# Fused image-and-text embedding with two layers on one Trainium2 core: the second half of the ternary down weights is made behind the low part of pair 0's turned rows, and its temporary moves from the squares' tile to the weight stage

## The chip, the cores and the metric

The kernel runs on one core of a Trainium2 chip. The metric is the device time of one execution in microseconds, taken as the median of several executions. The engines are named as the profile names them: PE is TensorE (PEld its weight loads), DVE is VectorE, ACT is ScalarE, POOL is GpSimd and SP is SyncE, which here only issues DMAs.

## What is computed

The reference embeds 32 images and 32 texts, runs a first layer (attention and a ternary feed-forward part) and then a second layer (a recurrent scan and a mixture of experts). The change touches the first layer's feed-forward weights alone:

```python
def _ternary_linear(x, w):
    alpha = jnp.mean(jnp.abs(w))
    w_t = jnp.sign(w) * (jnp.abs(w) > 0.5 * alpha).astype(w.dtype)
    w_q = w + jax.lax.stop_gradient(w_t - w)
    rms = jnp.sqrt(jnp.sum(x * x, axis=-1, keepdims=True)) / jnp.sqrt(jnp.asarray(d, x.dtype))
    return jnp.einsum('bsd,fd->bsf', x / (rms + EPS), w_q)
h = jax.nn.gelu(_ternary_linear(x, w_up), approximate=False)      # w_up: 1024 x 256
return _ternary_linear(h, w_down)                                 # w_down: 256 x 1024
...
h = h + _L0_attn_ref(_layernorm(h, axis=-1), L0_attn_wq, L0_attn_wk, L0_attn_wv)
h = h + _L0_ffn_ref(_layernorm(h, axis=-1), L0_ffn_w_up, L0_ffn_w_down)
```

## The kernel before

Three parts run one after the other: part A is layer 0, part B the recurrent part of layer 1, part C its experts. The change is in part A (`part_a`), which works on 16 pairs of batch elements. A pair is 384 rows of 256 values, held as 3 tiles of 128 rows. Matrices are multiplied as a high and a low part: ACT writes the high part out of PSUM, DVE the difference, and PE multiplies with both.

Each engine runs the same hand-written list of steps, `order` (L169), once per turn `g` of a software pipeline. `run` (L183) walks the list; `offset` says which pair a step works on: offset 0 is pair g, offset 1 (the default) pair g + 1, offset 2 pair g + 2, and steps of pairs that don't exist are left out. The turns -4 to 1 are written out, a hardware loop runs the middle ones, and the last four are written out again. Within an engine the list is the order; between engines only semaphores hold.

The feed-forward weights are made ternary on DVE, in two parts of 1024 columns each (`ternary`, L468). A part is two instructions: L478 writes (-w > threshold) as 0 or 1 into a temporary, `tern_tmp`, and L481 writes (w > threshold) minus that into `ternary_up` or `ternary_down`. `tern_tmp` lies in the first 1024 columns of `gelu_sq`, the tile into which ACT writes the squares of the gelu outputs from turn 0 on. Both parts of the down weights are made in turn -1, one behind the other, between `t_split` (which writes tT_lo of pair 1) and `scale2` (which normalises pair 0's rows for the feed-forward part). PE needs them at `down` of pair 0 in turn 0, where it waits for `w_sum` 4 (L747 to L749).

Around that place the pair 0 rows go this way, through all engines, in turn -1: DVE `scale2` (L664, L667, L671) writes x2_normed; PE `x2T` (L699) turns it into PSUM; ACT `x2_split` (L454) writes x2T_hi, and DVE `x2_split` (L541) x2T_lo. Between them stands DVE's `max` of pair 1 (L601, L605), for which ACT's `exp` of pair 1 (L438) waits, and PE's `tok` of pair 2 too, since it writes over the scores. Turn 0 goes on with `tok` of pair 2 (L688), `pT` of pair 1 (L827, behind ACT's exp) and the first `up` of pair 0 (L688), which needs x2T_lo. DVE's first step in turn 0 is `patch_split` of pair 3 (L537), which waits for tok of pair 2, the reader of patches_hi.

`weight_stage` is a tile of 2048 columns into which the patch weights (columns 0 to 1535) and the value weights (1536 to 2047) land before they are split. Its first 1024 columns are last read by DVE's first L531, at the start of part A. `fill` (L711) has PE do idle transposes at some places of the first turns; none stands ahead of x2T.

Of the kernel before, what the change touches and what calls it, by code (L numbers as in the profile page):

```python
# [71 lines left out]
def part_a(nc, W, io, consts):  # L72
    with ExitStack() as ctx:
        def sb(name, shape, dt=F32):
            return ctx.enter_context(nc.sbuf_tensor(name, shape, dt))
# [5 lines left out]
        stage = sb("weight_stage", [P, 4 * DI])  # L81
# [30 lines left out]
        sq = sb("gelu_sq", [P, DEEP, GT])  # L112
# [3 lines left out]

        flat_act = act[:].rearrange("p a b -> p (a b)")
        wq, wk = (flat_act[:, i * DC * D:(i + 1) * DC * D].rearrange("p (a b) -> p a b", a=DC) for i in range(2))
        tern_tmp = sq[:].rearrange("p a b -> p (a b)")[:, 0:1024]
        vec, soft = sb("channel_vectors", [P, 3, IC]), sb("softplus", [P, 7, IC])  # L120
        ms, rms = sb("rms_mean", [P, TILES]), sb("rms_root", [P, TILES])
        rden, rscale = sb("rms_den", [P, TILES]), sb("rms_scale", [P, TILES])
# [25 lines left out]
        for src, hi, lo in ((io["tokW"], tok_h, tok_l), (io["wvT"], wv_h, wv_l)):  # L148
            cols = flat(hi).shape[1]
            for a in range(0, cols, 1024):  # L150
                b = min(cols, a + 1024)
# [11 lines left out]
        order = """ids_load exp gelu_table tok merge pT up.0 up.1 patch_split patch_load emb pT_split root1 gelu.0 gelu.1 v  # L163
# [4 lines left out]
        order = [(w.split(".")[0], int((w + ".0").split(".")[1])) for w in order]  # L168
# [8 lines left out]
        for m, behind in enumerate((("turn_win", 0), ("up", 4), ("down", 2), ("down", 2), ("down", 2), ("down", 2), ("down", 2), ("down", 2))):  # L177
# [2 lines left out]
                at += 1  # L180
            order_last.insert(at, ("fold", m))

        def run(eng, piece, prepare=None):  # L183


            def step(g, sl, half, order=order):
                if prepare is not None and isinstance(g, int):
                    prepare(g)
                for kind, k in order:
                    off = offset.get(kind, 1)  # L190
                    if not isinstance(g, int) or 0 <= g + off < G:
                        piece(kind, k, g + off, (sl + off) % 2, half + (sl + off) // 2)

            for g in (-4, -3, -2, -1, 0, 1):
                step(g, g % 2, g // 2)
            with eng.Fori(1, G // 2 - 2) as half_:
                step(2 * half_, 0, half_)
                step(2 * half_ + 1, 1, half_)
            for g in range(G - 4, G):
                step(g, g % 2, g // 2, order_last if g == G - 1 else order)  # L200
# [38 lines left out]
        def _(sp):  # L239
# [27 lines left out]
            def piece(kind, k, n, sl, half):  # L267
# [7 lines left out]
                if kind == "h2" and k == TILES - 1:  # L275
                    sp.wait_ge(s["h2_done"], TILES * (n + 1))
                    for j in range(2):
                        sp.dma_start(io["h2"][2 * n + j, 0:N_IMG, :],
                                     h[j * N_IMG:(j + 1) * N_IMG, sl, 0, :]).then_inc(s["stored"], 16)
                        sp.dma_start(io["h2"][2 * n + j, N_IMG:T, :], h[:, sl, 1 + j, :]).then_inc(s["stored"], 16)  # L280

            run(sp, piece, prepare)
            sp.wait_ge(s["rows_out"], 16)
            sp.wait_ge(s["raw_in"], 48)
# [3 lines left out]
        def _(pool):  # L288
# [36 lines left out]
            def piece(kind, k, n, sl, half):  # L325
# [26 lines left out]
                if kind == "root2":  # L352
# [7 lines left out]
                                            ALU.pow).then_inc(s["ln2_roots"], 1)  # L360

            run(pool, piece, prepare)

        @block.scalar
        def _(sc):
# [26 lines left out]
            def piece(kind, k, n, sl, half):  # L392
# [58 lines left out]
                if kind == "x2_split":  # L451
                    sc.wait_ge(s["x2T_done"], n + 1)
                    wait(sc, s["up_done"], FC * n)
                    nc.scalar.activation(x2_h[:], XT[:, :, 0:GT], ACT.Copy).then_inc(s["x2_hi"], 1)  # L454

            run(sc, piece, prepare)

        @block.vector
# [1188 lines left out]
def program(nc, io):  # L1647
    with ExitStack() as ctx:
# [24 lines left out]
        both = ctx.enter_context(ExitStack())  # L1673
        W.ps = both.enter_context(nc.psum_tensor("psAB", [P, 8, 512], F32))
        part_a(nc, W, io, consts)

        E = Names()
# [69 lines left out]
```

## Time and profile before

| | us |
|---|---|
| median of 3 executions | 978.78 |
| lowest and highest of them | 977.89, 979.78 |
| the profiled execution, its own time | 980.27 |
| its span, first to last instruction | 978.5 |
| PE busy in the span | 936.2 (96%) |
| DVE busy | 791.5 (81%) |
| ACT busy | 593.9 (61%) |
| POOL busy | 544.8 (56%) |

A row of the timeline is a group of like instructions: start in us from the span's start, us it took, engine, line, operation, what is written from what, its shape, how many; in brackets the idle time of the engine just before it, with what ended it. PE's rows overlap, as matmuls are pipelined: the distance of their starts is the pace. Names in the profile stand without numbers, so `ln_den` may be ln2_den and `x_normed` may be x2_normed; the lines tell them apart.

### The profile page before, as it was taken

What the parts mean: (1) busy time and instruction counts of PE and PEld (TensorE: products, weight loads), DVE (VectorE), ACT (ScalarE), POOL (GpSimd) and SP (SyncE); (2) the same over time, 40 slices, a digit from 0 to 9 for tenths busy, and PEclk for the clock granted to TensorE, in tenths of its full rate; (3) what the DMA queues carried; (4) which work ended last, traced back from release to release, by engine and by line L of the source; (5) the groups of instructions that cost most, each with busy time, mean ns of one, the idle gap of its engine ahead of it and who ended that gap; (6) DMA issues with size and microseconds to landing.
All of it is one profiled execution on the core that took longest, in us unless ns stands there. A gap on an engine that the chain in (4) does not pass through costs nothing. (4 is left out here: it accounts for less than half of the span.)

```text
span 978.5 us, 19836 instructions
## 1 busy us (share of the span) xinstructions
PE 936.2 (96%) x6016; PEld 838.5 (86%) x6016; DVE 791.5 (81%) x2380; ACT 593.9 (61%) x1182; POOL 544.8 (56%) x674
## 2 busy tenths in 40 slices
PE   6889999999999999988899999999999999998998
PEld 6789999999999999875678888888888888887887
DVE  4878777777877777774589999999999988996787
ACT  2356666666666666664766767666677666752442
POOL 4156666666666776544445545554554466542673
PEclk9999999999999999999999999999999999999999
DMA  6001111111111113003699999999999999984220
GB/s 225 18 28 44 45 44 44 43 43 43 43 43 43 43 39 146 17 17 107 95 145 152 158 151 159 152 151 152 165 156 172 181 164 153 149 136 84 103 65 23
DMA packets 63021, 96.36 MB, mean 98 GB/s; under 512 B 12372, under 2 KB 32988, under 8 KB 62300
## 3 DMA queue, kind: packets, MB, share of 16 engines
q1 hardware_dynamic: 61396, 91.19, 50.4%
q0 software_dynamic: 1536, 4.20, 1.4%
q8 instruction: 37, 0.61, 0.3%
q14 instruction: 44, 0.36, 0.2%
q10 hardware_dynamic: 8, 0.00, 0.0%
HBM read 31.90 MB, written 13.11 MB: 46 GB/s over the span
## 5 line engine op out<-in xcount | busy, mean ns | idle before, releaser
L334 POOL TENSOR_TENSOR gelu_lo<-gelu_out,gelu_hi 128x384 fp32r<-128x384 f32 x124 | 146.0, 1206 | 29.1 <-DVE gelu_hi L549 28.7
L1058 POOL TENSOR_TENSOR B_y<-B_scan_in,B_states 128x512 f32<-128x512 f32 x47 | 60.7, 1291 | 80.2 <-ACT B_states L1147 80.2
L752 PE MATMUL psAB<-ternary_down,gelu_hi 128*128 128x256 f32 x384 | 96.8, 290 | 5.2 <-POOL gelu_lo L334 4.4
L688 PE MATMUL psAB<-x2T_hi,ternary_up 128*128 128x384 f32 x256 | 92.7, 362 | 0.8 <-DVE residual L678 0.6
L752 PE MATMUL psAB<-ternary_down,gelu_lo 128*128 128x256 f32 x384 | 93.3, 281 | 0.0
L688 PE MATMUL psAB<-x2T_lo,ternary_up 128*128 128x384 f32 x256 | 86.2, 337 | 0.0
L1336 PE MATMUL psAB<-Win_hi,B_x_hi 128*128 128x512 f32 x192 | 83.6, 435 | 0.0
L752 PEld LDWEIGHTS psAB<-ternary_down,gelu_hi 128*128 128x128 f32 x384 | 72.2, 188 | 9.6 <-POOL gelu_lo L334 8.0
L1070 POOL TENSOR_TENSOR B_decayed_u<-B_scan_in 128x512 f32<-128x512 f32 x48 | 62.3, 1297 | 29.6 <-DMA B_scan_in<-B_stage 26.6
L1243 DVE SCALAR_TENSOR_TENSOR psAB<-B_decayed_u,psAB 128x128 f32<-128x128 f32 x192 | 67.9, 354 | 13.3 <-PE psAB L1348 11.7
L1348 PEld LDWEIGHTS psAB<-B_partial_dots,B_minus_same_batch 128*128 128x128 f32 x384 | 65.1, 190 | 14.5 <-DVE B_partial_dots L1227 4.4
L1336 PE MATMUL psAB<-Win_hi,B_x_lo 128*128 128x512 f32 x192 | 75.5, 393 | 0.0
L1336 PE MATMUL psAB<-Win_lo,B_x_hi 128*128 128x512 f32 x192 | 75.3, 392 | 0.0
L752 PEld LDWEIGHTS psAB<-ternary_down,gelu_lo 128*128 128x128 f32 x384 | 72.4, 189 | 0.0
L1064 POOL TENSOR_TENSOR B_v_scale<-B_half_vv,half_powers 128x1 f32<-128x1 f32 x48 | 26.5, 551 | 77.9 <-ACT B_v_squared L1168 74.2
L403 ACT ACTIVATE gelu_out<-psAB 128x384 f32<-128x384 f32 x128 | 62.7, 490 | 10.5 <-PE psAB L688 10.2
L1227 DVE CUSTOM_DVE_ANT_0 B_products<-B_scan_in,psAB 128x128 f32<-128x128 f32 x192 | 55.1, 287 | 13.4 <-DVE psAB L1243 7.8
L1232 DVE TENSOR_TENSOR psAB<-psAB,B_scan_in 128x128 f32<-128x128 f32 x192 | 57.5, 299 | 6.5
L568 DVE TENSOR_TENSOR gelu_sq_sum<-gelu_sq_sum,gelu_sq 128x384 f32<-128x384 f32 x105 | 61.1, 582 | 1.7
L1348 PE MATMUL psAB<-B_partial_dots,B_minus_same_batch 128*128 128x1 f32 x384 | 54.6, 211 | 4.0 <-DVE B_partial_dots L1227 3.7
L318 POOL TENSOR_TENSOR patches_lo<-patches,patches_hi 128x768 fp32r<-128x768 f32 x16 | 29.7, 1855 | 50.7 <-DVE patches_hi L537 50.5
L390 ACT ACTIVATE gelu_sq<-gelu_out 128x384 f32<-128x384 f32 x112 | 57.3, 528 | 0.0
(275 smaller groups left out, 3346.2 us busy)
## 6 DMA issues: line engine op xcount, KB each, us to landing
B_scan_in<-B_stage SPq DMA_DIRECT2D x192, 256.0 KB, 6.9
patches<-in_patches SPq DMA_DIRECT2D x16, 384.0 KB, 3.1
B_residual<-layer_out SPq DMA_DIRECT2D x48, 128.0 KB, 4.2
out_dram<-B_residual SPq DMA_DIRECT2D x48, 128.0 KB, 3.6
layer_out<-residual SPq DMA_DIRECT2D x32, 128.0 KB, 1.8
raw_Win<-in_experts SPq DMA_DIRECT2D x3, 768.0 KB, 4.3
raw_Wl<-in_experts SPq DMA_DIRECT2D x3, 768.0 KB, 4.1
layer_out<-residual SPq DMA_DIRECT2D x32, 64.0 KB, 2.0
```

Source lines behind the costliest of these rows:

```text
L334: nc.gpsimd.tensor_tensor(act_l[:, k, :], act[:, k % DEEP, :], act_h[:, k, :].bitcast(F32), ALU.subtract).then_inc(s["ffn_lo"], 1)
L390: nc.scalar.activation(out, act[:, k % DEEP, :], ACT.Square).then_inc(s["sq_done"], 1)
L403: nc.scalar.activation(act[:, k % DEEP, :], ps[:, 6 + k % 2, 0:GT], ACT.Gelu).then_inc(s["gelu_done"], 1)
L568: nc.vector.tensor_tensor(sqsum[:], sqsum[:], sq[:, k % DEEP, :], ALU.add).then_inc(s["sqsum_done"], 1)
L688: last = nc.tensor.matmul(out, a, b, start=(n == 0), stop=(n == len(terms) - 1))
L752: last = nc.tensor.matmul(ps[:, 6 + k // 2, (k % 2) * D:(k % 2 + 1) * D], x[:, c, k * P:(k + 1) * P], dn_w[:, c, :], start=(c == 0 and x i ...
L1058: nc.gpsimd.tensor_tensor(y[:, j % 2], ring[:, j % R_RING, :, GATE, :], hs[:, j % 2], ALU.mult).then_inc(s["y"], 1)
L1070: nc.gpsimd.tensor_tensor(lu[:, j % 2], ring[:, j % R_RING, :, LAM, :], ring[:, j % R_RING, :, U, :], ALU.mult).then_inc(s["lu"], 1)
L1232: nc.vector.tensor_tensor(state(j, k), state(j, k), ring[:, j % R_RING, k, DRIVE, :], ALU.subtract).then_inc(s["scan"], 1)
L1243: nc.vector.scalar_tensor_tensor(out=state(i, k), in0=lu[:, i % 2, k, :], scalar=dot[:, t % 2:t % 2 + 1], in1=state(i, k), op0=ALU.mult, o ...
L1336: last = nc.tensor.matmul(out, a, b, start=(not biased and ks[0] == 0 and n == 0), stop=(ks[-1] == DC - 1 and n == len(terms) - 1), skip_g ...
L1348: nc.tensor.matmul(dot[:, t % 2:t % 2 + 1], minus[:], part[:, t % 2:t % 2 + 1], start=True, stop=True).then_inc(s["dot"], 1)
```

## The change

One extra list, `order_fill`, is `order` with the second part of the down weights, `("tern_down", 1)`, taken out and put at the end. It is used in turn -1 alone, the only turn in which that step does anything. `tern_tmp` becomes the first 1024 columns of `weight_stage`; this holds for all four ternary parts.

```diff
-        tern_tmp = sq[:].rearrange("p a b -> p (a b)")[:, 0:1024]
+        tern_tmp = stage[:, 0:1024]
...
+        order_fill = [w for w in order if w != ("tern_down", 1)] + [("tern_down", 1)]
...
-                step(g, g % 2, g // 2)
+                step(g, g % 2, g // 2, order_fill if g == -1 else order)
```

No instruction is added or taken away, and PE, ACT, POOL and SP have the same lists as before. On DVE, two instructions move. The first place is DVE in turn -1 between tT_lo of pair 1 and pair 0's normalised rows; before:

```order
L541 TENSOR_TENSOR tT_lo<-psAB,tT_hi 128x768
L472 TENSOR_SCALAR half_alpha<-psAB 128x1
L478 TENSOR_SCALAR gelu_sq<-raw_Wv,half_alpha 128x1024
L481 SCALAR_TENSOR_TENSOR ternary_down<-raw_Wv,half_alpha,gelu_sq 128x1024
L478 TENSOR_SCALAR gelu_sq<-raw_Wv,half_alpha 128x1024
L481 SCALAR_TENSOR_TENSOR ternary_down<-raw_Wv,half_alpha,gelu_sq 128x1024
L664 SCALAR_TENSOR_TENSOR ln2_den<-ln2_roots 128x3
```

The same place in the changed kernel (its lines are numbered 3 higher):

```order
L544 TENSOR_TENSOR tT_lo<-psAB,tT_hi 128x768
L475 TENSOR_SCALAR half_alpha<-psAB 128x1
L481 TENSOR_SCALAR weight_stage<-raw_Wv,half_alpha 128x1024
L484 SCALAR_TENSOR_TENSOR ternary_down<-raw_Wv,half_alpha,weight_stage 128x1024
L667 SCALAR_TENSOR_TENSOR ln2_den<-ln2_roots 128x3
```

One of the two pairs of ternary instructions is gone from ahead of ln2_den, the first step of the normalisation.

The second place is DVE at the end of turn -1 and the start of turn 0; before:

```order
L605 TENSOR_SCALAR neg_max<-row_max 128x3
L541 TENSOR_TENSOR x2T_lo<-psAB,x2T_hi 128x768
L537 CAST patches_hi<-patches 128x768
L610 TENSOR_TENSOR embedded<-psAB,patch_bias 128x256
L614 BN_STATS ln_stats<-embedded 128x6 x3
```

And in the changed kernel:

```order
L608 TENSOR_SCALAR neg_max<-row_max 128x3
L544 TENSOR_TENSOR x2T_lo<-psAB,x2T_hi 128x768
L481 TENSOR_SCALAR weight_stage<-raw_Wv,half_alpha 128x1024
L484 SCALAR_TENSOR_TENSOR ternary_down<-raw_Wv,half_alpha,weight_stage 128x1024
L540 CAST patches_hi<-patches 128x768
L613 TENSOR_TENSOR embedded<-psAB,patch_bias 128x256
L617 BN_STATS ln_stats<-embedded 128x6 x3
```

The moved pair now stands between x2T_lo of pair 0 and the split of pair 3's patches.

## Rows read from the trace of the kernel before

**Rows 1.** A window of 25 us: length, busy us of each engine (instructions), PEclk, DMA.

```profile
217.00:242.00 25.00, 24.80 (x186) 24.02 (x186) 19.62 (x57) 16.20 (x35) 17.36 (x17) 1.00 0.15 42
```

**Rows 2.** Timeline of PE, end of turn -1 to the middle of turn 0.

```profile
54.50 1.19 PE L699 MATMUL psAB<-ident,x_normed 128*128 128x128 f32 x6 [3.25 <-DVE x_normed L671]
55.62 0.55 PE L688 MATMUL psAB<-tokW_hi,patches_hi 128*128 128x256 f32 x1
...
59.05 0.71 PE L827 MATMUL psAB<-ident,probs 128*128 128x128 f32 x5
...
65.35 0.28 PE L688 MATMUL psAB<-v_hi,probT_hi 128*128 128x256 f32 x1
```

**Rows 3.** Timeline of DVE over the same stretch.

```profile
50.99 0.75 DVE L478 TENSOR_SCALAR gelu_sq<-raw_Wv,half_alpha 128x1024 f32<-128x1024 f32 x1
...
52.98 0.15 DVE L664 SCALAR_TENSOR_TENSOR ln_den<-ln_roots 128x3 f32<-128x3 f32 x1
...
53.39 1.06 DVE L671 TENSOR_SCALAR x_normed<-residual,ln_moments,ln_scale 128x256 f32<-128x256 f32 x3
...
55.39 0.08 DVE L601 DVE_READ_ACCUMULATOR2_ANT row_max<- 128x1 f32 x1
...
56.57 0.96 DVE L541 TENSOR_TENSOR x2T_lo<-psAB,x2T_hi 128x768 fp32r<-128x768 f32 x1 [0.89 <-ACT x2T_hi L454]
59.31 0.56 DVE L537 CAST patches_hi<-patches 128x768 fp32r<-128x768 f32 x1 [1.79 <-PE psAB L688]
...
62.52 0.60 DVE L549 CAST gelu_hi<-gelu_out 128x384 fp32r<-128x384 f32 x2
64.15 0.96 DVE L541 TENSOR_TENSOR v_lo<-psAB,v_hi 128x768 fp32r<-128x768 f32 x1 [1.03 <-ACT v_hi L379]
```

**Rows 4.** Timeline of ACT: pair 0's high part, pair 1's exp, the table load.

```profile
55.73 0.81 ACT L454 ACTIVATE x2T_hi<-psAB 128x768 fp32r<-128x768 f32 x1 [7.93 <-PE psAB L699]
56.43 0.50 ACT L438 ACTIVATE probs<-probs,neg_max 128x256 f32<-128x256 f32 x1
...
58.02 1.28 ACT L433 ACT_TABLE_LOAD   x1
...
59.79 0.71 ACT L379 ACTIVATE probT_hi<-psAB 128x640 fp32r<-128x640 f32 x1 [0.27 <-PE psAB L827]
```

**Rows 5.** Timeline of POOL: pair 0's roots, then pair 3's low patches.

```profile
47.91 1.76 POOL L359 TENSOR_TENSOR ln_roots<-ln_pair,half_powers 128x6 f32<-128x6 f32 x1
...
59.96 1.86 POOL L318 TENSOR_TENSOR patches_lo<-patches,patches_hi 128x768 fp32r<-128x768 f32 x1 [8.08 <-DVE patches_hi L537]
```

**Rows 6.** Timeline of PE, other places: the same steps at full pace.

```profile
41.88 0.82 PE L699 MATMUL psAB<-ident,x_normed 128*128 128x128 f32 x6
42.53 1.26 PE L716 MATMUL psAB<-ident 128*128 128x128 f32 x10
...
81.79 0.36 PE L688 MATMUL psAB<-tokW_hi,patches_hi 128*128 128x256 f32 x1
...
84.03 0.71 PE L827 MATMUL psAB<-ident,probs 128*128 128x128 f32 x5
```

**Rows 7.** Timeline of PE: three other idle stretches of the first turns.

```profile
10.93 0.35 PE L688 MATMUL psAB<-tokW_hi,patches_hi 128*128 128x256 f32 x1 [1.88 <-DVE tokW_lo L531]
...
21.03 1.33 PE L699 MATMUL psAB<-ident,x_normed 128*128 128x128 f32 x5 [4.24 <-DVE x_normed L628]
...
32.54 0.36 PE L688 MATMUL psAB<-tokW_hi,patches_hi 128*128 128x256 f32 x1 [1.43 <-DVE row_max L601]
```

**Rows 8.** Windows around PE's idle stretches, columns as in rows 1.

```profile
31.00:33.00 2.00, 0.57 (x5) 0.49 (x5) 1.69 (x8) 0.36 (x1) 0.00 (x0) 1.00 0.00 0
...
54.40:58.00 3.60, 3.50 (x17) 3.20 (x18) 2.20 (x9) 2.27 (x7) 0.00 (x0) 0.57 0.00 0
...
490.00:500.00 10.00, 8.38 (x36) 6.59 (x36) 7.18 (x27) 5.38 (x11) 4.03 (x8) 0.83 1.09 151
```

**Rows 9.** Waits of PE's weight loads from 60 to 450 us: total, times, longest.

```profile
PEld psAB L752 <- POOL gelu_lo L334: 8.0, 17, 1.2
```

## The prediction

> **What bounds the kernel now.** I read the table of windows first. In the middle turns PE is busy 24.80 of 25 us, at clock 1.00, while DVE has 19.62 and POOL 17.36 [rows 1]; the windows from 67 to 367 us read alike. So in the steady turns PE is the bound, and whatever makes PE start turn 0 earlier should reach the end of the kernel whole, since every later wait, transfers included, hangs on steps of these turns. What is left to win lies in the first turns, where PE still waits for one pair's chain. The timeline of PE shows the place: the transposes of pair 0's rows start at 54.50, after 3.25 us idle that DVE's x2_normed ended [rows 2]; so the work before, the scores of pair 1, ended at 51.25. DVE is not waiting in that time, it is working: the second ternary part stands at 50.99, ln2_den at 52.98, x2_normed at 53.39 [rows 3]. The idle stretch costs a second time, behind it. PE takes 1.12 us from the first transpose to the first tok matmul (54.50 to 55.62) [rows 2], where the same six transposes take 0.65 (41.88 to 42.53) elsewhere [rows 6]; and the 18 tok matmuls take 3.43 us (55.62 to 59.05) [rows 2] against 2.24 (81.79 to 84.03) [rows 6]. The reason is the granted clock, 0.57 in this window of 3.6 us [rows 8]: the lower level, 1.2 GHz, for nearly all of it.
>
> **Taking the second part out of the front.** It holds DVE from 50.99 to 52.98, that is 1.99 us [rows 3]. With it gone ln2_den can start at 50.99 if its input is there: POOL's roots end at 49.67 (47.91 + 1.76) [rows 5], so nothing else is late, and there is 1.32 us of room. x2_normed starts at 51.40, the row maxima end at 53.48 (55.39 + 0.08 - 1.99) [rows 3], and neg_max, one small instruction, follows. PE's transposes start at 52.51 instead of 54.50, after 1.26 us idle. Shift so far: **1.99 us**.
>
> **The clock.** PE has idled 1.88 and 1.43 us elsewhere in these turns [rows 7], and the window around the latter shows clock 1.00 [rows 8]; the tok matmuls behind it run at the full pace. After 4.24 us the transposes were slow, five in 1.33 us [rows 7], and after 3.25 us they were slow too [rows 2]. A gap of 1.26 us is nearest to the first two, so I take the full clock. The two ends are 0 (the clock falls all the same) and the whole difference. At the full clock: transposes 52.51 to 53.16. tok of pair 2 must wait for the row maxima, which end at 53.48; behind the same wait the matmul came 0.14 us later in the rows I have (55.47 to 55.62) [rows 2, 3], so it starts at 53.62 and its 18 matmuls end at 53.62 + 2.24 = 55.86. pT also needs ACT's exp. x2T_hi started 1.23 us after the first transpose at the slow pace [rows 2, 4]; less the 0.47 that the transposes save, it is at 52.51 + 0.76 to 0.86 = 53.3 to 53.4, the exp follows 0.70 later at 54.1 (it stood behind x2T_hi without idle time, not behind neg_max), and ends 1.59 later (56.43 to 58.02) [rows 4], at 55.7. So pT starts at 55.86 instead of 59.05: **shift 3.19 us**, with exp 0.1 to 0.2 us ahead of being the bound. The clock's part is 1.2 us of it.
>
> The Trainium skill ("TensorE: Matmul & The Clock Gate", Part 1) says that the monitor that gates the clock is free-running and that its transition point differs from one execution of a kernel to the next. No row here can show that, since one execution was profiled. By it the 3.25 us gap may leave the clock up in some executions of the kernel before, and for those the change would bring only the first term; the second rival below has that time.
>
> **What the part costs in its new place.** x2T_lo waits for x2T_hi as before and runs from about 54.2 to 55.1. Then the part takes its 1.99 us, to 57.1, on a stretch where DVE used to stand idle 1.79 us for tok of pair 2 (57.5 to 59.31) [rows 3]. At the full clock tok is done at 55.9, so patches_hi of pair 3 is now late by DVE's own work: 57.1 instead of 56.1, a shift of 2.2 us where PE has 3.2. What queues behind it on DVE: embedded and its moments, probT_lo, the first gelu_hi, then v_lo, for which PE's pv waits. DVE had 1.03 us idle ahead of v_lo (waiting for v_hi) [rows 3]; the lag is 1.0 us. So gelu_hi ends at 63.12 - 2.2 = 60.9 and v_hi, shifted 3.2, ends at 64.15 - 3.2 = 60.95: v_lo comes on time to within 0.1 us, and pv (65.35) [rows 2] had v_lo at 65.11, another 0.2 us of room. I take 0 for it; the end on the other side is 0.3. POOL's patches_lo follows patches_hi (59.96) [rows 5] and is read a turn later. ACT's probT_hi stood 0.27 us idle and then at 59.79 [rows 4]; now the table load ends at 55.7 + 1.49 = 57.2, where it shifts by 2.6 us and not 3.2, but the gelus after it end in a wait for PE's v, as before. The down weights are needed at 72.0 at the earliest, 12 us after they are done.
>
> **The temporary's move** costs nothing: same size, same type, the same DVE instructions, in a tile whose last reader on DVE is long past. It is what lets the part stand next to turn 0's squares. ACT, POOL and SP issue what they issued, in the same order; no DMA moves past anything.
>
> **Sum.** 3.19 - 0 to 0.3, about 3.2 us. Against the profiled execution: 980.27 - 3.2 = 977.1. The profiled execution lies 1.49 above the median of the three; taken off the median, 978.78 - 3.2 = 975.6.
>
> **Rivals.**
> 1. *Only the shift* (1.99 us, 976.8). Either the clock falls in the changed kernel too: two short gaps, 1.26 and 0.46 us with 0.65 us of work between, add up to 1.72, near the 1.88 that left it up. Or it had not fallen in the executions that make the median of before; for this speaks that they spread over 1.9 us (977.89 to 979.78) and that the profiled one, which did fall, is above them all. Against: 3.25 us idle is nearer to the 4.24 that was slow than to 1.88 [rows 7].
> 2. *Most of the gain is used up in turn 0* (about 978.4). DVE is the engine with the least room: v_lo is on time to 0.1 us. If the moved pair took 4.0 us instead of 2.0 beside ACT's and PE's work, pv would wait about 2.0 - 0.2, and 3.2 - 1.8 leaves 1.4; a second such wait at gelu_hi or at x_normed would take another 1.0. Against it: DVE idles 5 us in each turn [rows 1], and the pair took the same time wherever it stood in the rows I read.
> 3. *Slower, by a lasting lag.* DVE and POOL enter turn 0 one us later against PE than before. PE's weight loads wait for gelu_lo 17 times for 8.0 us together, 0.47 each, at most 1.2 [rows 9]. If the lag stayed and each of 15 pairs waited 1.2, that is 15 x 0.73 = 11 us, less 3.2: 7.8 slower, 986.6. It decides only from the point where DVE's idle share of a turn is under the 1.0 us lag; it has 5.4 us, and POOL 7.6 [rows 1]. The lag should be gone within turn 0.
> 4. *The change does nothing*: ln2_den would wait for POOL's roots. They are 1.3 us early even against the new place [rows 5]; practically excluded.
>
> A further spread has nothing to do with the place: between 490 and 500 us the clock is 0.83 [rows 8], a second stretch of lower clock at the change to part B of (1 - 0.83) x 10 / 0.5 = 3.4 us. Whether it falls there may differ, which is worth up to 3.4 / 2 = 1.7 us either way in one execution and some tenths in a median.
>
> **How the numbers follow.** The forecast (both terms, 3.2 us, own range 975.0 to 976.4) has 0.55, the shift alone 0.27 (976.4 to 977.4), the gain mostly used up or gone 0.14 (977.8 to 978.9), slower 0.04. The range has to hold 8 in 10: from 974.6, the forecast less the spread of medians, to 977.6, which takes in nearly all of the second case. A measurement of this kernel can tell about 0.2%, 1.96 us, from no change. The forecast is beyond it nearly always (0.53 of 0.55); the shift alone lies just on it (0.14 of its 0.27); from the third case 0.02 comes to it. Faster 0.69, same 0.27, slower 0.04.
>
> **What the profile of the changed kernel would show.** PE's idle time ahead of the first L699 of x2T near 1.26 us; x2_normed near 51.4; clock 1.00 between 52.5 and 56; tok behind row_max at 53.6; pT near 55.9. The moved pair right behind x2T_lo, about 2.0 us long, patches_hi behind it without idle time and near 57.1. v_lo near 60.9 and pv near 62.2. PE in windows of 25 us as busy as before. Wrong would be: a clock of 0.5 behind the short gap (rival 1), PE idle ahead of pv for DVE's v_lo (rival 2), or waits for gelu_lo above 0.47 us in the middle pairs (rival 3).

## The result and the profile after

| | before | changed |
|---|---|---|
| median of 19 executions, us | 980.53 | 978.01 |
| lowest and highest | 977.67, 983.92 | 974.09, 980.08 |
| the profiled execution, its own time | 980.27 | 977.63 |
| its span | 978.5 | 975.7 |

The ratio is 0.9974, with a 95% interval of 0.9964 to 0.9985: the change takes 2.5 us off, between 1.5 and 3.5. The 3.2 us that were forecast lie within that interval. The time that was forecast, 975.6 us with a range up to 977.6, does not: the 978.01 us of the changed kernel are 0.4 above it. The medians of 19 are of both kernels; the three executions of before that the forecast was anchored to (median 978.78) lay 1.75 us under the 19.

Timeline of PE in the changed kernel, around the place; it answers rows 2 (columns as there):

```profile
48.62 0.38 PE L691 MATMUL psAB<-xT_hi,tT_hi 128*128 128x256 f32 x1 [0.63 <-DVE tT_lo L544]
...
52.17 0.88 PE L702 MATMUL psAB<-ident,x_normed 128*128 128x128 f32 x6 [1.14 <-DVE x_normed L674]
...
53.29 0.36 PE L691 MATMUL psAB<-tokW_hi,patches_hi 128*128 128x256 f32 x1 [0.24 <-DVE row_max L604]
...
55.52 0.71 PE L830 MATMUL psAB<-ident,probs 128*128 128x128 f32 x5
...
61.83 0.28 PE L691 MATMUL psAB<-v_hi,probT_hi 128*128 128x256 f32 x1
...
70.33 0.38 PE L755 MATMUL psAB<-ternary_down,gelu_hi 128*128 128x256 f32 x1
...
71.28 0.39 PE L755 MATMUL psAB<-ternary_down,gelu_hi 128*128 128x256 f32 x1 [0.45 <-POOL gelu_lo L337]
```

PE idles 1.14 us ahead of the transposes where it idled 3.25 [rows 2]; tok waits 0.24 us for the row maxima, as forecast, and its 18 matmuls take 2.23 us (53.29 to 55.52) instead of 3.43. The last two rows lie in the first down. Its matmuls usually start 0.12 us apart; here one starts 0.43 us behind the one before it (69.90 to 70.33) and a second 0.73 us (70.55 to 71.28), since the weight loads wait for POOL's gelu_lo. The kernel before had one such place, 0.31 us long (73.66 to 73.97), in a down that started at 72.12:

```profile
73.97 0.38 PE L752 MATMUL psAB<-ternary_down,gelu_hi 128*128 128x256 f32 x1
```

Timeline of DVE over the same stretch; it answers rows 3:

```profile
51.05 1.06 DVE L674 TENSOR_SCALAR x_normed<-residual,ln_moments,ln_scale 128x256 f32<-128x256 f32 x3
...
53.93 0.96 DVE L544 TENSOR_TENSOR x2T_lo<-psAB,x2T_hi 128x768 fp32r<-128x768 f32 x1 [0.58 <-ACT x2T_hi L457]
54.80 0.75 DVE L481 TENSOR_SCALAR weight_stage<-raw_Wv,half_alpha 128x1024 f32<-128x1024 f32 x1
55.58 1.28 DVE L484 SCALAR_TENSOR_TENSOR ternary_down<-raw_Wv,half_alpha,weight_stage 128x1024 fp32r<-128x1024 f32 x1
56.78 0.55 DVE L540 CAST patches_hi<-patches 128x768 fp32r<-128x768 f32 x1
...
60.62 0.96 DVE L544 TENSOR_TENSOR v_lo<-psAB,v_hi 128x768 fp32r<-128x768 f32 x1
61.50 1.93 DVE L631 TENSOR_SCALAR x_normed<-embedded,ln_moments,ln_rstd 128x256 f32<-128x256 f32 x3
```

The moved pair takes 1.98 us (54.80 to 56.78) and patches_hi and v_lo follow without idle time. The last row was not foreseen: the three instructions take 1.93 us. The same three took 1.05 in the trace before:

```profile
65.02 1.05 DVE L628 TENSOR_SCALAR x_normed<-embedded,ln_moments,ln_rstd 128x256 f32<-128x256 f32 x3
```

Windows of the changed kernel, columns as in rows 1:

```profile
52.10:55.60 3.50, 3.19 (x25) 2.98 (x26) 2.85 (x11) 2.50 (x8) 0.00 (x0) 1.00 0.13 37
404.00:417.00 13.00, 11.16 (x60) 10.63 (x60) 6.17 (x18) 7.47 (x18) 3.14 (x4) 0.74 0.11 31
480.00:492.00 12.00, 10.07 (x42) 7.99 (x42) 7.82 (x28) 5.75 (x14) 3.60 (x7) 0.86 1.08 142
```

The clock stays up behind the shorter gap, 1.00 against the 0.57 of rows 8. But this execution had a lower clock between 404 and 417 us, where the profiled execution of before had 1.00:

```profile
404.00:417.00 13.00, 11.09 (x82) 10.36 (x81) 9.46 (x27) 8.11 (x18) 2.97 (x4) 1.00 0.11 31
```

Matmul by matmul, the changed kernel's lead over that trace shrinks there from 3.0 to 0.2 us, and comes back to 1.6 us where the other had its fall (490 to 500 us, rows 8) and to 2.5 at the end. What the change gives where it acts is therefore read below from places in the trace, not from two times.

**One zero for all.** The start of the kernel scatters, so places are counted from the first score matmul of pair 1 (48.84 us in the first trace of before, 48.62 in that of the changed kernel), which stands ahead of everything that the change touches. The rows that this table is read from are PE's: the first transpose of x2T, the first tok matmul, pT (the transposes of the probabilities), pv (the probabilities times v), the first down matmul of pair 0 and of the 14th pair. "Fill" is more idle transposes at one place, "halves" and "quarters" are the ternary part in pieces; each has its section below.

| us from that zero | zero | x2T | tok | pT | pv | down, pair 0 | down, 14th |
|---|---|---|---|---|---|---|---|
| before | 48.84 | 5.66 | 6.79 | 10.21 | 16.51 | 23.29 | 349.74 |
| before, again (b2) | 48.45 | 5.66 | 6.78 | 10.30 | 16.84 | 23.63 | 350.11 |
| temporary only (e2) | 47.88 | 5.66 | 6.85 | 9.90 | 16.20 | 22.99 | 349.45 |
| before with fill (e1) | 48.11 | 5.66 | 6.78 | 9.00 | 15.30 | 22.07 | 348.26 |
| changed | 48.62 | 3.55 | 4.67 | 6.90 | 13.21 | 19.98 | 346.97 |
| changed, again (a2) | 49.67 | 3.56 | 4.67 | 6.89 | 13.20 | 21.12 | 346.86 |
| without the part (e3) | 49.72 | 3.55 | 4.67 | 6.90 | 13.20 | 19.97 | 346.49 |
| part twice (e5) | 49.55 | 3.56 | 4.68 | 6.89 | 15.09 | 23.12 | 349.14 |
| halves, one in turn 0 (e6) | 50.14 | 3.55 | 4.67 | 6.90 | 14.00 | 20.85 | 347.44 |
| quarters and fill (e8) | 47.88 | 2.77 | 3.89 | 6.13 | 13.72 | 20.58 | 347.06 |
| halves in turn -1 (e9) | 48.31 | 3.55 | 4.67 | 6.92 | 13.26 | 20.04 | 346.93 |
| halves and fill (e10) | 47.84 | 3.55 | 4.67 | 6.91 | 13.26 | 20.04 | 346.84 |
| changed with fill (e11) | 48.03 | 3.56 | 4.68 | 6.89 | 13.20 | 21.13 | 346.86 |

### The profile page after: what moved, and what is told of

Read it like the earlier page. It is cut to its first block and busy times, and to the rows that moved or that the text cites. A ratio compares the mean times of both kernels' runs of the same rounds, so it can differ in the third digit from the quotient of the medians.

```text
span 975.7 us, 19836 instructions
## 1 busy us (share of the span) xinstructions
PE 937.6 (96%) x6016; PEld 840.1 (86%) x6016; DVE 790.8 (81%) x2380; ACT 594.0 (61%) x1182; POOL 545.0 (56%) x674
## 5 line engine op out<-in xcount | busy, mean ns | idle before, releaser
L691 PEld LDWEIGHTS psAB<-x2T_hi,ternary_up 128*128 128x128 f32 x256 | 48.6, 190 | 10.6 <-ACT gelu_out L406 8.0
```

The lines of the kernel that those rows point to most:

```text
L691: last = nc.tensor.matmul(out, a, b, start=(n == 0), stop=(n == len(terms) - 1))
```

## The experiments

The theory: the change gives the shift (2 us) and the clock term behind it (1.2 us), and the lag of DVE in turn 0 takes about 0.5 us of them back; the rest of the difference between any two executions is the clock elsewhere. The rivals: the clock falls in some executions only; the temporary has a price; the loss in turn 0 is POOL's own. Each kernel was profiled once, unless a second profile is named.

### The kernel before, again

> The unchanged kernel, profiled a second time. Question: does the lower clock follow the 3.25 us idle stretch ahead of the transposes in every execution? My theory (the clock term of 1.2 us is there in each execution): the 18 tok matmuls behind the stretch take 3.4 us again, at a granted clock of about 0.57. Rival (the clock falls there in some executions only): they take 2.2 to 2.6 us in this one. Elsewhere, at 486 to 498 us and at 400 to 415 us, I expect the stretches of lower clock to lie differently from the first profile, as the trace of the changed kernel has one of 6.8 us at 407 that the first trace of before has not.

The lower clock came again, and later behind the gap (the gap is 50.87 to 54.12):

```profile
54.00:57.60 3.60, 3.24 (x19) 3.04 (x20) 2.21 (x9) 2.56 (x8) 0.00 (x0) 0.75 0.00 0
...
55.80:59.20 3.40, 3.40 (x19) 3.40 (x18) 1.10 (x2) 2.99 (x9) 0.00 (x0) 0.50 0.00 0
```

So tok starts at full pace here and ends slow: the lower clock lies at 7.3 to 10.8 us of the count, where the first trace has it from 6.1 us on. It reaches into turn 0: pT at 10.30, the first down at 23.63. In the temporary-only kernel it lay earlier (from 5.3 us on; 0.56 in 53.4 to 57.0 us). Three profiles with the 3.25 us gap, three falls, at three offsets. The rival falls as far as three can tell. The executions that were timed say the same from further off. A stretch of 3.4 us at half the clock takes 0.0017 off the mean granted clock of an execution; that mean is 0.9905 over 12 executions of the kernel before (those of the last section of experiments) and 0.9927 over the 19 of the changed kernel, so one such stretch or a little more is gone on average (single executions scatter from 0.988 to 0.995 and from 0.990 to 0.998). It does not tell where. The Trainium skill ("TensorE: Matmul & The Clock Gate", Part 1) calls the monitor free-running, with a transition point that varies; the offsets agree, but the further step that the prediction made of it, that some executions escape, no trace here shows. (The time that it gives for them, 976.8 us, stands under the first rival of the prediction and not under the second.) The other half of the expectation held too: between 404 and 417 us this one had 0.87 where the first had 1.00.

### The clock term by itself: fill ahead of x2T

```diff
-                    ("t", 1): 10, ("score", 1): 10}
+                    ("t", 1): 10, ("score", 1): 10, ("x2T", 0): 24}
```

> The kernel before with 24 idle transposes on PE ahead of the x2T of pair 0 (the same fill that other places have), and nothing else: PE is kept busy over the 3.25 us stretch, while DVE's work stays as it was. It measures the clock term by itself. My theory: the transposes still start near 54.5, tok near 55.6 and takes 2.24 us instead of 3.43, pT starts near 57.85, 1.2 us earlier than before; DVE's x_normed of pair 2 takes 1.05 us (no lag on DVE), and the 1.2 us are still there at pair 0's first down matmul and at 390 us. Rival (PE is held by ACT's exp there and not by its own pace): pT starts within 0.5 us of 59.05.

```profile
50.36 2.78 PE L716 MATMUL psAB<-ident 128*128 128x128 f32 x24
...
53.78 0.87 PE L699 MATMUL psAB<-ident,x_normed 128*128 128x128 f32 x6 [0.63 <-DVE x_normed L671]
...
54.90 0.36 PE L688 MATMUL psAB<-tokW_hi,patches_hi 128*128 128x256 f32 x1 [0.24 <-DVE row_max L601]
...
57.11 0.71 PE L827 MATMUL psAB<-ident,probs 128*128 128x128 f32 x5
```

With nothing on DVE moved, pT is at 9.00 instead of 10.21, 1.21 us earlier, which is the forecast term to 0.01. Against the three kernels with the gap the first down matmul is 0.92, 1.22 and 1.56 us earlier, by where the lower clock fell in them. pT starts 2.21 us behind tok, so PE's own pace bounds this stretch and not exp; the rival is out. DVE's x_normed of pair 2 takes 1.05 us, as expected. At the 14th pair it is 1.2 to 1.9 us ahead. This kernel's one time was 976.58 us, beside 978.19 for before; single executions say little.

### The temporary alone

> The kernel before with the ternary temporary in the weight stage and the order as it was. My theory: nothing changes, each part takes 2.0 us and every start in part A stays within 0.1 us, once the first matmuls' start is taken off (the idle stretch of 3.25 us ahead of the transposes stays). Rival (the new place of the temporary has a price or a gain of its own): the two instructions take another time than 0.75 and 1.28 us.

```profile
50.03 0.75 DVE L478 TENSOR_SCALAR weight_stage<-raw_Wv,half_alpha 128x1024 f32<-128x1024 f32 x1
50.82 1.28 DVE L481 SCALAR_TENSOR_TENSOR ternary_down<-raw_Wv,half_alpha,weight_stage 128x1024 fp32r<-128x1024 f32 x1
52.02 0.15 DVE L664 SCALAR_TENSOR_TENSOR ln_den<-ln_roots 128x3 f32<-128x3 f32 x1
```

0.75 and 1.28 us, ln2_den 1.99 us behind the part's start: the new place of the temporary costs and gives nothing. x2T is at 5.66 as before. "Within 0.1 us" held up to tok; behind it the place of the lower clock makes 0.3.

### The changed kernel, again

> The changed kernel unchanged, profiled a second time. Counted from the first score matmul of pair 1 (its place in the trace is the zero of all that follows), the first profile of it had the transposes at 3.55, tok at 4.67, pT at 6.90, the first down matmul at 19.98 and that of the 14th pair at 346.97; the first of before had 5.66, 6.79, 10.21, 23.29, 349.74. My theory (the local gain is the same in each execution, the rest of the scatter is the clock elsewhere): the same numbers within 0.1 us up to the first down matmul and within 0.3 at the 14th pair, x_normed 1.93 us, no lower clock between 48 and 70 us. Rival (the short gaps of 1.14 and 0.24 us cost the clock in some executions): a stretch of lower clock there.

Everything up to pv repeats within 0.01 us, and the 14th pair within 0.11; the clock is 1.00 from 48 to 75 us. Two misses: the first down matmul is at 21.12, not 19.98, and x_normed took 1.75 us, not 1.93. The wait has only moved: here PE waits 0.88 us ahead of t of pair 2 for xT_lo, and then not in down. Two casts of DVE took 1.16 and 1.17 us instead of 0.35:

```profile
64.95 1.16 DVE L552 CAST gelu_hi<-gelu_out 128x384 fp32r<-128x384 f32 x1
...
66.50 1.17 DVE L552 CAST gelu_hi<-gelu_out 128x384 fp32r<-128x384 f32 x1
```

with POOL at the same time:

```profile
64.64 1.25 POOL L337 TENSOR_TENSOR gelu_lo<-gelu_out,gelu_hi 128x384 fp32r<-128x384 f32 x1 [0.82 <-DVE gelu_hi L552]
66.19 1.26 POOL L337 TENSOR_TENSOR gelu_lo<-gelu_out,gelu_hi 128x384 fp32r<-128x384 f32 x1 [0.29 <-DVE gelu_hi L552]
```

Each cast starts 0.31 us into a gelu_lo of POOL and ends 0.2 us behind its end (64.64 + 1.25 = 65.89, and 66.11). Either way the next pair is reached at the same place.

### Without the moved part

```diff
+                        nc.gpsimd.memset(dn_w[:, FC // 2:, :].bitcast(F32), 1.0)
...
-        order_fill = [w for w in order if w != ("tern_down", 1)] + [("tern_down", 1)]
+        order_fill = [w for w in order if w != ("tern_down", 1)]
```

> The changed kernel without the moved part: the second half of the ternary down weights is not computed but filled with ones by POOL at the start (part of the output is therefore another). It asks what the part costs in its new place. In the changed kernel DVE came 1.0 us late against PE into turn 0, its x_normed of pair 2 took 1.93 us instead of 1.05 while POOL ran gelu_lo, gelu_hi 2 came late, and PE waited for gelu_lo at down for 0.9 us in two pieces instead of 0.2; the shift against before went from 3.2 us at tok to 2.7 at the next pair. My theory (it is the lag): without the part patches_hi starts near 55.6, x_normed takes 1.05 us, PE waits at down as before (0.2 to 0.3), and the shift stays 3.2 us up to 390 us. Rival (the loss comes from PE being early against POOL whatever DVE does): x_normed is back to 1.05 or not, but PE waits 0.7 to 0.9 us for gelu_lo at down again.

```profile
56.88 0.56 DVE L541 CAST patches_hi<-patches 128x768 fp32r<-128x768 f32 x1 [0.90 <-PE psAB L692]
...
61.71 0.96 DVE L545 TENSOR_TENSOR v_lo<-psAB,v_hi 128x768 fp32r<-128x768 f32 x1 [1.03 <-ACT v_hi L383]
62.59 1.05 DVE L632 TENSOR_SCALAR x_normed<-embedded,ln_moments,ln_rstd 128x256 f32<-128x256 f32 x3
```

PE and SP wait for three ternary parts here instead of four. DVE stands idle 0.90 us ahead of patches_hi and 1.03 ahead of v_lo, x_normed is back at 1.05, PE's waits in down are back to the size of before (0.31 between two starts, as before, instead of 0.43 and 0.73), and the 14th pair comes at 346.49. Against 346.97 and 346.86 the part costs 0.37 to 0.48 us in its new place; the loss is DVE's lag and not POOL's own. The absolute 55.6 for patches_hi was missed, mostly because the kernel's start came 1.1 us later; from the zero it is 7.17, where the changed kernel has 8.17.

### The part twice

```diff
+                if k == 3:
+                    nc.vector.tensor_scalar(tern_tmp, raw[:, col], -1.0, half_alpha[:, n:n + 1], ALU.mult,
+                                            ALU.is_gt).then_inc(s["w_abs_parts"], 1)
+                    v.wait_ge(s["w_abs_parts"], 3)
+                    nc.vector.scalar_tensor_tensor(out=out[:, col], in0=raw[:, col], scalar=half_alpha[:, n:n + 1],
+                                                   in1=tern_tmp, op0=ALU.is_gt, op1=ALU.subtract).then_inc(s["w_abs_parts"], 1)
+                    v.wait_ge(s["w_abs_parts"], 4)
```

> The changed kernel with the moved part done twice in its new place (4.0 us of DVE instead of 2.0, the same result). It doubles the lag. Lag theory: nothing hides it now, so v_lo is late by 2.0, PE's pv waits about 1.8 us for it, and the 14th pair's down is later than in the changed kernel by 1.3 to 2.0 us (counted from the scores of pair 1: 348.3 to 349.0 instead of 346.97). Rival (a lag on DVE is taken up by DVE's idle 5 us of a turn, as the changed kernel's loss of 0.48 us at 2.0 us of work suggests): less than 0.7 us later.

```profile
64.63 0.36 PE L698 MATMUL psAB<-v_hi,probT_hi 128*128 128x256 f32 x1 [1.73 <-DVE v_lo L551]
```

Another 2.1 us of DVE bring PE 1.73 us of waiting for v_lo, and the 14th pair to 349.14, 2.2 us later than in the changed kernel: the lag theory, a little above its range. The first 2.0 us cost 0.4, the second 2.2, since nothing was left to hide them. Rival 2 of the prediction has its mechanism right and its price nearly: it left 1.4 us of the gain behind pv, and 1.42 are left there (16.51 to 15.09); with a second wait it left 0.4, and 0.60 are left at the 14th pair. The condition for it (4.0 us of work) is simply not met by the changed kernel.

### Other places for it

> The changed kernel with the moved part in two halves of 512 columns: the first behind x2T_lo, the second in turn 0 behind the second gelu_hi, ahead of v_lo, where DVE had idled 1.03 us. Without the part altogether the 14th pair's down came at 346.49 from the scores of pair 1, with it at 346.97. Lag theory: patches_hi comes 1.0 us earlier than in the changed kernel, x_normed still starts at about the same time as there, since the second half stands ahead of it, so it may meet POOL's gelu_lo again; the 14th pair's down between 346.5 and 347.0. Rival (any half in turn 0 costs its full 1.0 us): above 347.2.

> A version meant to be faster: the down weights in four pieces of 512 columns (about 1.0 us each): the first where it was, the second between the row maxima and x2T_lo, the third behind x2T_lo, the fourth in turn 0 ahead of v_lo. In addition 48 instead of 16 idle transposes ahead of xT of pair 0, where PE idles 4.24 us and loses the clock at 21 us. Theory: the roots are ready 1.2 us ahead of ln2_den in the changed kernel, so x2_normed and the transposes start 0.95 to 1.0 us earlier (2.6 from the scores of pair 1 instead of 3.55), and the 14th pair's down comes at 346.0 instead of 346.97; the start up to the scores is 1.0 to 1.3 us shorter through the clock. Rival (the fourth piece's lag and the later x2T_lo eat it): the 14th pair's down at 346.7 or later.

> The changed kernel with the moved part in two halves of 512 columns, both still in turn -1: one between neg_max and x2T_lo, where DVE idles 0.58 us for ACT, one behind x2T_lo. From the profiles so far a half takes 1.2 us. Theory (the loss of the changed kernel is DVE's lag against PE in turn 0, through x_normed meeting POOL's gelu_lo): patches_hi starts 0.3 to 0.4 us earlier than in the changed kernel (7.8 instead of 8.16 us from the first score matmul of pair 1), x_normed of pair 2 takes 1.3 to 1.9 us, and the first down matmul of the 14th pair lies at 346.6 to 346.9, against 346.97 and 346.86 in the changed kernel and 346.49 without the part. Rival (up of pair 0 now waits for x2T_lo, which comes 0.6 us later): up starts later than 7.37 from that zero, and the 14th pair lies above 347.0.

The edit of the last of the three, which the other two resemble:

```diff
+        order_fill = [w for w in order if w != ("tern_down", 1)] + [("tern_down", 2)]
+        order_fill.insert(order_fill.index(("max", 0)) + 1, ("tern_down", 1))
...
+                    a, b = ((0, 1024), (1024, 1536), (1536, 2048))[k]
+                    ternary(1, a, b, 2 + k)
```

In both kernels with a piece in turn 0 the rival came true, and the theory did not: PE waits for v_lo, 0.62 us in the halves kernel and 1.08 us in the quarters kernel:

```profile
64.14 0.36 PE L695 MATMUL psAB<-v_hi,probT_hi 128*128 128x256 f32 x1 [0.62 <-DVE v_lo L545]
```

```profile
61.59 0.36 PE L696 MATMUL psAB<-v_hi,probT_hi 128*128 128x256 f32 x1 [1.08 <-DVE v_lo L546]
```

The 14th pair is at 347.44 in the halves kernel (above 347.2, as the rival said), 0.95 us behind the kernel without the part. The piece in turn 0 is not only late there, it also takes longer. Its second instruction took 1.39 us, where the same form takes 0.75 in turn -1; DVE's row and POOL's in the halves kernel:

```profile
61.74 1.39 DVE L485 SCALAR_TENSOR_TENSOR ternary_down<-raw_Wv,half_alpha,weight_stage 128x512 fp32r<-128x512 f32 x1
```

```profile
61.37 2.63 POOL L339 TENSOR_TENSOR gelu_lo<-gelu_out,gelu_hi 128x384 fp32r<-128x384 f32 x2
```

The two gelu_lo of POOL took 1.99 us in the changed kernel. v_lo starts at 12.91 us of the count instead of 12.00, so 0.91 late, and 0.64 of this is that longer instruction. The quarters kernel shows the same 1.39 us. It does bring the transposes 0.78 us forward (2.77 instead of 3.55), less than the 0.95 that was expected, and loses it ahead of pv: 347.06, above the rival's 346.7.

Halves around x2T_lo start patches_hi at 7.87 instead of 8.17, shorten x_normed to 1.59 us, and end where the changed kernel does: 346.93 and, with fill, 346.84 against 346.97 and 346.86. Of 346.6 to 346.9, which was expected, the first is just outside and the second inside; the difference to the changed kernel is within what two profiles of one kernel differ by. Of the rival's two signs one came (up of pair 0 at 7.41 instead of 7.37), the other (above 347.0) did not.

### The fall at the start, and a faster kernel

```diff
-            fill = {("tok", 0): 40, ("xT", 0): 16, ("t", 0): 10, ("score", 0): 10, ("pv", 0): 10, ("xT", 1): 4,
+            fill = {("tok", 0): 40, ("xT", 0): 48, ("t", 0): 10, ("score", 0): 10, ("pv", 0): 10, ("xT", 1): 4,
```

> The changed kernel with 48 instead of 16 idle transposes ahead of xT of pair 0, where PE idles about 4.2 us at 17 to 21 us. In nine profiles the clock was low for 3.4 or 6.8 us near there, and the first score matmul of pair 1 started anywhere from 47.9 to 50.1 us. Theory (that scatter is the clock): no lower clock between 16 and 48 us, and that matmul starts at 47.5 to 48.0. Rival (the scatter comes from the first DMAs or DVE): it starts above 48.3 with the clock up.

> Both together: the halves of 512 columns and 48 idle transposes, timed. The sum of the terms against the kernel before: 2.8 us in the median for the change, 0.1 to 0.3 for the halves, 0.8 to 1.5 for the clock at the start, so 3.7 to 4.6 us less than before, a ratio of 0.9953 to 0.9962. Rival (the clock falls elsewhere in exchange): 0.9975, as the changed kernel.

Windows from 17 to 29 us, first of the changed kernel's second profile, then with the fill:

```profile
17.00:29.00 12.00, 8.11 (x40) 7.71 (x40) 8.04 (x10) 1.62 (x2) 3.96 (x3) 0.72 0.21 57
```

```profile
17.00:29.00 12.00, 10.26 (x80) 9.22 (x78) 9.62 (x13) 1.62 (x2) 3.98 (x3) 1.00 0.19 55
```

With the fill the clock stays up, and the zero of the table lies at 47.84 to 48.03 in the three kernels that have it (47.5 to 48.0 was expected), against 47.88 to 50.14 in the ten profiles without. These ten part by the clock: where it was low for 6.8 us at the start, in four of them, the zero lies at 49.55 to 50.14; where it was low for 3.4 us, in six, at 47.88 to 48.84. The lowest of them, 47.88, is the temporary-only kernel, whose lower clock lay at 12 to 16 us, ahead of the long idle stretch and not behind it. Halves and fill together, timed: 974.25 us median of 7 (972.52 to 978.16) beside 981.13 for before (12 executions), ratio 0.9944, interval 0.9922 to 0.9965. That is under the forecast 0.9953 to 0.9962, with the forecast inside the interval. It is the fastest kernel here. By the 14th pair the halves give it nothing that can be told from zero. Its zero lies 1.0 us ahead of the mean of the ten profiles without fill, while its ratio is 0.3% (2.9 us) under that of the changed kernel; where the other 1.9 us come from is not shown. The two ratios were measured apart, and their intervals touch.

## Why the prediction was right or wrong

**What bounds the kernel**: right. Of the 3.31 us that PE had won at the first down (23.29 to 19.98) it still had 2.77 at the 14th pair; the rest went in the waits named below, and PE's windows in the middle turns read as before.

**The shift**, 1.99 us: mechanism and place right, 2.11 us measured (5.66 to 3.55, each time). ln2_den stands 1.99 us behind the second part's start, as the rows said, but the second part itself had waited for the end of the first, which ln2_den need not: in the changed kernel it starts 1.20 us behind the start of the first part's L484 (49.45 to 50.65), where the second part started 1.32 behind it (49.67 to 50.99).

**The clock term**, 1.2 us: right, 1.21 measured with the fill; at the first down it is 0.9 to 1.6, by where in tok and turn 0 the lower clock lies. The six transposes and the 18 matmuls of tok ran at full pace in all nine profiles with a gap of 1.15 us or less. pT came at 6.90, 3.31 us earlier; 3.19 was forecast. ACT's exp ended 0.15 us ahead of it, as worked out.

**The lag**, "I take 0 for it; the end on the other side is 0.3": a step that was mis-sized. v_lo was on time, exactly as argued (60.62, and pv without a wait). What the step did not look at stands one instruction further. POOL's first two gelu_lo hang on gelu_hi, which did lag by 1.0 us, so they lay over x_normed of pair 2, and it took 1.93 us instead of 1.05. Rows of the changed kernel, POOL and DVE, the latter for the first of the three instructions:

```profile
60.64 1.99 POOL L337 TENSOR_TENSOR gelu_lo<-gelu_out,gelu_hi 128x384 fp32r<-128x384 f32 x2
```

```profile
61.50 1.28 DVE L631 TENSOR_SCALAR x_normed<-embedded,ln_moments,ln_rstd 128x256 f32<-128x256 f32 x1
```

The 1.28 us instruction, 0.41 elsewhere, ends 0.15 us behind POOL's second gelu_lo (62.63 and 62.78). The Trainium skill ("SBUF — State Buffer", Who interferes with whom) says of DVE's copies, casts and tensor_scalars in their two-port mode and GpSimd's instructions that "whoever issues first gets the shared pair for the whole instruction; the other fully blocks". No row tells in which mode these instructions ran. The trace agrees with the rule for the two casts of the second profile: each started 0.31 us into a POOL instruction and ended 0.2 us behind it. For x_normed it agrees only in part. It started inside the first gelu_lo, but waited for the second too, whose row starts 0.11 us behind its own:

```profile
61.61 1.01 POOL L337 TENSOR_TENSOR gelu_lo<-gelu_out,gelu_hi 128x384 fp32r<-128x384 f32 x1
```

The cost at PE was 0.37 to 0.48 us where the prediction had 0 to 0.3, and the statement that the lag "should be gone within turn 0" came true only after it had cost that.

**The sum against the profiled execution**: 977.1 forecast, 977.63 measured. Near, though in part by luck: the two profiled executions had their lower clock at different places behind 400 us.

**The sum against the median**: the step that put the time outside the range. The term "taken off the median, 978.78" was mis-sized: 19 executions, the same three among them, give 980.53. The prediction noted that the profiled execution lay 1.49 above the median of three, and explained it by this one gap, which might not have cost the clock in the three (rival 1); but the profiled execution had been the ordinary one. With the same 3.2 us the anchor of 19 gives 977.3, inside the range. The prediction allowed "some tenths in a median" for the clock elsewhere; the median of three was off by 1.75 us. Why the three lay low is open: they were not profiled. The 3.2 us themselves were somewhat too large. The terms as the traces show them are 2.11 + 1.21 less about 0.5, and the 14th pair has 2.77; the medians of 19 differ by 2.52, and their interval holds both this and 3.2.

**The rivals.** The shift alone is out: the clock fell in all three profiles with the long gap, in none of nine with the short one. The gain used up: 0.4 to 0.5 us of it are, by a neighbour of the mechanism that was named. The lasting lag is out: at the 14th pair the changed kernel stands as far ahead (2.77 us) as at the second (2.76). Nothing at all is out too: ln2_den did not wait for the roots. The forecast of faster by more than 0.2% is carried by the estimate of 0.26%; its interval, 0.15% to 0.36%, reaches below that mark.

## What to carry to other kernels

When work is moved out of a stretch in which another engine idles, look whether the idle time counts twice: as itself and as the lower clock behind it. Here it did for 3.25 us of idle time and did not for 1.14; an idle fill at that place measures the second term alone. In the new place, follow not only the engine that now comes late but the pairs of instructions of DVE and POOL that slide over one another: the same ternary half took 1.23 us of DVE in one place and 1.87 in the other. And before a change of 0.3% is put against a median of three, look at how far single executions spread: here the median of three was 1.75 us off, for an effect of 2.5.

## What the runs showed of the hardware that was not expected

A TENSOR_SCALAR of DVE took 1.28 us instead of 0.41, a SCALAR_TENSOR_TENSOR 1.39 instead of 0.75, and CASTs 1.16 and 1.17 instead of 0.35, when they started inside a POOL instruction. In the trace before, a cast of the same form started 0.31 us into a POOL instruction too, as the two slow ones did, and took 0.35. There POOL's instruction was the longer one, 2.27 us instead of the usual 1.01:

```profile
66.42 2.27 POOL L334 TENSOR_TENSOR gelu_lo<-gelu_out,gelu_hi 128x384 fp32r<-128x384 f32 x1 [1.26 <-DVE gelu_hi L549]
```

```profile
66.73 0.35 DVE L549 CAST gelu_hi<-gelu_out 128x384 fp32r<-128x384 f32 x1
```

So one of the two pays, and the order of the starts in these rows does not say which.

The lower clock can come with much shorter pauses than the 3.25 us one. Ahead of pT and up in the last turns PE pauses 1.21 and 0.63 us in every profile; the second trace of before shows them so:

```profile
409.58 0.74 PE L827 MATMUL psAB<-ident,probs 128*128 128x128 f32 x5 [1.21 <-DVE x2T_lo L541]
...
410.94 0.69 PE L688 MATMUL psAB<-x2T_hi,ternary_up 128*128 128x384 f32 x1 [0.63 <-DVE residual L678]
```

At this pair of pauses the clock fell in 7 of the 13 profiles (0.74 in the window 404 to 417 us of the changed kernel, 0.87 in that of before's second trace) and stayed at 1.00 in 6. In five of the seven it had fallen before the second pause ended, as in the changed kernel, where the row behind that pause starts at 407.97 and the clock is 0.50 from 407.40 on:

```profile
407.40:413.00 5.60, 5.03 (x19) 5.03 (x20) 2.54 (x8) 2.08 (x5) 2.02 (x2) 0.50 0.25 72
```

It fell in 2 of the 4 profiles with the order of before and in 5 of the 9 with the changed one, so that nothing points to the change as a cause. Behind the changed kernel's own 1.14 and 0.24 us ahead of x2T and tok it fell in none of 9 (in one of these, the quarters kernel, the first pause was 0.35). So the prediction's nearest rows, a pause of 1.43 and one of 1.88 us without a fall, were less safe a bound than they looked; what decides between the executions was not tried.
